# Softmax division in the layout of the values product: inverted sums spread by DMA

## The chip, the cores and the metric

The kernel runs on one core of one Trainium2 chip. The time is the device time of one execution in microseconds, the median of a few runs.

## The reference

One transformer layer on x of shape 16 x 512 x 256. Sliding-window attention with 16 heads of 16 and a window of 128: for each block of 128 queries the keys are the block itself and the one before, the scores get a bias that depends on distance, softmax is taken over the keys, and the result is projected with `w_out`. Then residual and layer norm give x1. A gated recurrence runs over the 16 sequences of x1 (`T` is the sequence number, all 512 positions at once), and its final state `c` enters every output:

```
p = softmax(scores); o = einsum(p, v)
x1 = layernorm(x + o @ w_out.T)
c = sigmoid(x1[t] @ wf.T + c @ uf.T + bf) * c + sigmoid(... wi, ui, bi) * tanh(... wc, uc, bc)   # for t in 0..15
out = layernorm(x1 + tanh(x1 @ wo.T + c @ uo.T + bo))
```

## The kernel before, in words

All is fp32; products that need full precision are made of a high part (rounded, `fp32r`) and a low part (value minus high), three matmul passes each. ScalarE makes the high parts (`x_hi`, `qk_hi`, `ot_hi`, `x1_hi`, `c_hi`), VectorE mostly the low parts by `minus_hi` (L661: `x_lo`, `qk_lo`, `ot_lo`, `x1_lo`), GpSimd the low part of the state (L364).

**Pipeline.** `iteration(t)` on each engine works on several sequences at once: q and k of t+1, scores of t, values of t-1, output projection and layer norm of t-2, gates of t-3. An iteration has 16 *slots* (`attend(0)` to `attend(15)`); slot s makes raw scores for quad s // 4 (four heads) of sequence t (TensorE, L951, into the banks `MX`), whose row maxima VectorE takes (L689, into `max_q`), and, seven slots later, the masked scores of the same piece (L972), which ScalarE exponentiates (L448) into `Pt`. GpSimd cuts the window out of `Pt` (L347, L349). Between the slots stand the other products, written out by hand in the same order on each engine; every engine waits on semaphores.

**Rows through DRAM.** q and k parts are stored to `parts_dram` by SyncE (`parts_to_dram`, four DMAs of 256 KB for each of two chunks, L239) and read back stacked (`stack`, eight DMAs for each quad, L254). Row maxima are transposed by TensorE (L959), negated into `max_rows` (L454) and put into the stack by two DMAs (`max_to_stack`, L262). SyncE works through its list in order: a wait there holds back all that stands behind it.

**The division.** The values product (L986) gives four heads at once, 32 rows a head: 16 context rows, then the row of the softmax sums (a column of ones in `Vp`), for 512 queries. `ctx_out` (L459) copies it to the single buffer `ctx_raw`. `ctx_transpose` (L994) turns it with four matmuls, so that queries lie on partitions. `normalise` on VectorE takes the reciprocal of the 16 sums a partition (L698) and multiplies (L703) into `o_tok`. With all four quads done `o_transpose` (L1027, eight matmuls) turns back, and `ot_hi` and `ot_lo` make the two parts of `oT` for the projection with `Wout`.

**Start and end.** At the start SyncE loads all weights, ScalarE and GpSimd make their parts (`weights_hi`, L416; L340), and the first exponentials wait for the fifth of them. Behind the last iteration `last_sequences()` on each engine finishes the last sequences in an order of its own; then a second phase reads x1 back from DRAM into `ring` and makes the outputs with `Wo` (L1297).

The few lines around which the change turns:

```
c4 = bank[:, :].rearrange("p (n h d) -> p n h d", n=NB, h=4)
ve.reciprocal(rden..., c4[:, :, :, D]).then_inc(rden_done, 1)
o4 = o_tok[:, :, 4 * D * g:4 * D * (g + 1)]...
ve.tensor_tensor(o4, c4[:, :, :, 0:D], r4, ALU.mult).then_inc(o_done, 1)
```

## Time and profile before

| | |
|---|---|
| time, median of 3 runs | 994.17 us (993.75 to 994.33) |
| the profiled execution, its own time | 994.83 us |
| its span, first to last instruction | 992.7 us |
| mean granted TensorE clock | 0.955 |
| TensorE busy | 911.2 us, 92% |
| VectorE busy | 714.1 us, 72% |
| ScalarE busy | 574.8 us, 58% |
| GpSimd busy | 409.0 us, 41% |
| DMA, mean over the span | 131.86 MB, 133 GB/s |

The profile is of one execution. A busy share is taken over the whole span; a stretch of the views by time shows it for one part. "Idle before" is an engine's pause in front of an instruction, with what ended it. A granted clock of 1.00 is 2.4 GHz, 0.50 is 1.2 GHz.

### The profile page before, as it was taken

The numbers are of one execution on the slowest core, as the hardware profiler recorded it, in microseconds if no ns is written. First come the engines' busy times: TensorE is split into PE (matmuls) and PEld (weight loads), VectorE is DVE, ScalarE is ACT, GpSimd is POOL, SyncE is SP. The second block draws the span as 40 slices with busy tenths as digits, with TensorE's granted clock in tenths as the row PEclk, the third lists the DMA queues.
The fourth block names the chain that finished last, engine by engine and source line by source line (L and its number), as shares of the span: only waits on it lengthen the run. The fifth ranks groups of instructions, "written<-read, shape, count | busy, mean of one in ns | idle before, by whom it ended". The sixth has DMA issues, their size and how long they took to land. (4 is left out here: it accounts for less than half of the span.)

```text
span 992.7 us, 25986 instructions
## 1 busy us (share of the span) xinstructions
PE 911.2 (92%) x9500; PEld 749.7 (76%) x9500; DVE 714.1 (72%) x2795; ACT 574.8 (58%) x1167; POOL 409.0 (41%) x687
## 2 busy tenths in 40 slices
PE   3587889999999999999999999999999999989994
PEld 2365668888888888888888888888787876668884
DVE  7666677878787868787878787878787754337875
ACT  6044556565656565656565656565656554335786
POOL 6143343444535353535353535354444443001443
PEclk8586989999999999999999999999999989899998
DMA  7644454535454545353645454645444400131764
GB/s 265 164 124 127 131 139 132 151 122 156 124 151 128 145 134 150 123 154 125 153 128 151 128 143 137 149 131 147 133 121 138 119 23 22 44 106 46 215 204 131
DMA packets 93534, 131.86 MB, mean 133 GB/s; under 512 B 12128, under 2 KB 47584, under 8 KB 93408
## 3 DMA queue, kind: packets, MB, share of 16 engines
q1 hardware_dynamic: 93136, 129.95, 45.3%
q8 instruction: 76, 1.25, 0.5%
q14 instruction: 50, 0.41, 0.1%
q10 hardware_dynamic: 272, 0.26, 0.1%
HBM read 79.31 MB, written 50.33 MB: 131 GB/s over the span
## 5 line engine op out<-in xcount | busy, mean ns | idle before, releaser
L689 DVE CUSTOM_DVE_ANT_0 bank<-bank,mask 128x256 f32<-128x256 f32 (+1 forms) x1024 | 369.4, 423 | 130.7 <-PE bank L951 128.7
L448 ACT ACTIVATE Pt<-bank 128x512 f32<-128x512 f32 (+1 forms) x512 | 248.2, 536 | 193.4 <-PE bank L972 193.3
L347 POOL TENSOR_SCALAR_AFFINE_SELECT Pt<-Pt 128x512 f32<-128x512 f32 x256 | 170.4, 666 | 403.9 <-ACT Pt L448 403.9
L951 PE MATMUL bank<-Ks,Qs 59*128 59x256 f32 (+1 forms) x1024 | 148.2, 319 | 44.9 <-DVE max_q L689 31.3
L951 PEld LDWEIGHTS bank<-Ks,Qs 59*128 59x128 f32 x1024 | 107.3, 191 | 86.6 <-DVE max_q L689 42.5
L689 DVE DVE_READ_ACCUMULATOR2_ANT max_q<- 128x1 f32 x1024 | 144.9, 142 | 0.0
L349 POOL TENSOR_SCALAR_AFFINE_SELECT Pt<-Pt 128x384 f32<-128x384 f32 x256 | 144.7, 565 | 0.0
L986 PE MATMUL bank<-Pt,Vp 128*32 128x256 f32 (+1 forms) x2048 | 130.9, 377 | 0.0
L932 PE MATMUL bank<-x1T,Wg 64*128 64x512 f32 x960 | 127.9, 398 | 1.0 <-DVE o_tok L703 1.0
L932 PE MATMUL bank<-cT,Ug 64*128 64x512 f32 x960 | 125.7, 393 | 0.0
L972 PE MATMUL bank<-Qs,Ks 60*128 60x256 f32 (+1 forms) x1024 | 111.8, 271 | 0.7 <-ACT Pt L448 0.3
L986 PEld LDWEIGHTS bank<-Pt,Vp 128*32 128x32 f32 x2048 | 81.4, 116 | 31.9 <-issue 7.9
L932 PEld LDWEIGHTS bank<-cT,Ug 64*128 64x128 f32 x960 | 89.1, 184 | 18.2
L932 PEld LDWEIGHTS bank<-x1T,Wg 64*128 64x128 f32 x960 | 87.3, 185 | 18.9 <-DVE o_tok L703 1.4
L972 PEld LDWEIGHTS bank<-Qs,Ks 60*128 60x128 f32 x1024 | 94.7, 192 | 3.0 <-issue 1.3
L459 ACT ACTIVATE ctx_raw<-bank 128x512 f32<-128x512 f32 x64 | 38.2, 597 | 53.3 <-PE bank L994 50.7
L486 ACT ACTIVATE gate<-bank,bias_half 128x512 f32<-128x512 f32 x64 | 42.4, 685 | 42.2 <-PE bank L932 23.9
L920 PE MATMUL bank<-xT,Win 128*128 128x512 f32 x204 | 55.1, 423 | 7.9 <-DVE Win L661 7.9
L932 PE MATMUL bank<-Win,xT 64*128 64x256 f32 x768 | 54.6, 284 | 0.0
L920 PEld LDWEIGHTS bank<-xT,Win 128*128 128x128 f32 x204 | 40.1, 203 | 16.6 <-DVE Win L661 7.9
L661 DVE SCALAR_TENSOR_TENSOR qk_parts<-bank,qk_parts 128x512 fp32r<-128x512 f32 x64 | 42.5, 685 | 13.9 <-ACT qk_parts L431 13.9
L431 ACT ACTIVATE qk_parts<-bank 128x512 fp32r<-128x512 f32 x64 | 38.0, 593 | 23.0 <-PE bank L920 20.2
(111 smaller groups left out, 1354.7 us busy)
## 6 DMA issues: line engine op xcount, KB each, us to landing
parts_dram<-qk_parts SPq DMA_DIRECT2D x128, 256.0 KB
Qs<-parts_dram SPq DMA_DIRECT2D x128, 128.0 KB, 2.7
Ks<-parts_dram SPq DMA_DIRECT2D x128, 128.0 KB, 2.8
xt_raw<-in_xt SPq DMA_DIRECT2D x16, 512.0 KB, 4.5
Qs<-parts_dram SPq DMA_DIRECT2D x128, 64.0 KB, 2.7
Ks<-parts_dram SPq DMA_DIRECT2D x128, 64.0 KB, 2.7
x_res<-in_x SPq DMA_DIRECT2D x16, 512.0 KB, 3.9
x_dram<-y SPq DMA_DIRECT2D x16, 512.0 KB, 4.4
```

Source lines behind the costliest of these rows:

```text
L347: gp.affine_select(out=p4[:, :, 0:128], in_=p4[:, :, 0:128], compare_op=ALU.is_ge, fill=0.0, base=0, pattern=[[0, 4], [1, 128]], channel_m ...
L349: gp.affine_select(out=p4[:, 0:3, 128:256], in_=p4[:, 0:3, 128:256], compare_op=ALU.is_ge, fill=0.0, base=0, pattern=[[0, 3], [-1, 128]], ...
L448: sc.activation(probabilities(g, 2 * pair + odd)[:, S * a:S * a + n], SC[odd][:, 0:n], ACT.Exp).then_inc(exp_done, 1)
L459: sc.activation(ctx_raw[:, :], bank[:, :], ACT.Copy).then_inc(ctx_done, 1)
L486: ins = sc.activation(gate[:, k if k == 3 else which, :], bank[:, :], ACT.Tanh, bias=bias_half[:, which, j:j + 1], scale=0.5)
L661: return ve.scalar_tensor_tensor(out_, in_, scale, hi.bitcast(F32), op0=ALU.mult, op1=ALU.subtract)
L689: ins = ve.tensor_tensor_reduce(out=raw, in0=raw, in1=mask[:, keys], scale=1.0, scalar=MASKED, op0=ALU.add, op1=ALU.max, accum_out=max_q[: ...
L920: ins = te.matmul(out_, w, m, start=(first and n == 0), stop=(last and n == len(todo) - 1))
L932: ins = te.matmul(out_, w(r), m(r), start=(turn == 0 and opens and n == 0), stop=final, skip_group_check=True)
L951: ins = te.matmul(MX[odd][:, 256 * (n % 2):256 * (n % 2) + 256][:, keys], Qs[rows, 2 * g + pair, n * WIN:(n + 1) * WIN], Ks[rows, 2 * g + ...
L972: ins = te.matmul(SC[odd][:, 256 * (j % 2):256 * (j % 2) + width], Ks[rows, 2 * g + pair, j * WIN:(j + 1) * WIN], Qs[rows, 2 * g + pair, j ...
L986: ins = te.matmul(bank[32 * hh:32 * hh + 32, j * WIN:j * WIN + width], Vp[:, j, PITCH * h:PITCH * h + 32], probabilities(g, hh)[:, 256 * j ...
```

## The change

For the first 15 sequences the context is not turned on TensorE. ScalarE copies it to `ctx_raw` as before and stores it to DRAM from its own queue (`ctx_dram`, one DMA a quad). SyncE loads the rows of the contexts into `o_un`, in the layout in which `oT` is needed, and the rows of the sums into `den_q` (four DMAs). VectorE turns 32x32 blocks of the sums, inverts them and turns back; SyncE stores the inverses and reads them back 16 times each (`inv_den`); GpSimd multiplies. `ot_hi` and `ot_lo` now read `o_un` and stand one place later, behind slots 1 and 2. The last sequence goes the old way (`last_...`).

To make room: the low parts of x move from VectorE to GpSimd, and both parts of x are made an iteration earlier, in slots 11 and 12 (x of t+2 instead of t+1 in slots 1 and 2). `Wo` and `Uo` become parts of `Win`'s memory and are loaded and split at the end, not at the start.

```
+ def load_denominators(t):
+     sp.wait_ge(den_cleared, 1)
+     for g in range(QUADS): wait(sp, ctx_stored[g], 16, t, 16)
+     wait(sp, inv_stored, 16, t - 1, 16)
+     rows = ctx_dram[t % 2].rearrange("g (h r) (q i) -> q (g h) r i", r=2 * D, i=128)[:, :, D, :]
+     for q in range(4): sp.dma_start(den_q[32 * q:32 * q + H, :], rows[q]).then_inc(den_in, 16)
+ def load_contexts(t, c):
+     for g in (2 * c, 2 * c + 1): wait(sp, ctx_stored[g], 16, t, 16)
+     wait(sp, otlo_done, 2, t - 1, c + 1)
+     rows = ctx_dram[t % 2, 2 * c:2 * c + 2].rearrange("g (h r) s -> (g h) r s", r=2 * D)[:, 0:D, :]
+     sp.dma_start(o_un[:, c, :], rows).then_inc(o_un_in[c], 16)
+ def store_inverses(t):
+     wait(sp, inv_turned, 1, t, 1)
+     sp.dma_start(inv_dram[t % 2].rearrange("r (q i) -> q r i", i=128), den_q[:, :]).then_inc(inv_stored, 16)
+ def spread_inverses(t):
+     wait(sp, inv_stored, 16, t, 16)
+     for c in range(KC):
+         wait(sp, scaled_done, 2, t - 1, c + 1)
+         rows = inv_dram[t % 2, 8 * c:8 * c + 8]
+         sp.dma_start(inv_den[:, c, :], rows.unsqueeze(1).to_broadcast([8, D, S])).then_inc(inv_in[c], 16)
  # SyncE, iteration(t)
+ if now: stack(t, 2)
+ if by_rows: load_contexts(t - 1, 0)
  if real(t + 2): load_xt(t + 2)
  if now:
-     stack(t, 2)
      max_to_stack(t, 0)
...
+ if by_rows: load_denominators(t - 1)
  if n1: stack(t + 1, 0)
+ if by_rows: load_contexts(t - 1, 1)
  if now: max_to_stack(t, 2)
+ if by_rows:
+     store_inverses(t - 1)
+     spread_inverses(t - 1)
  if n1: parts_to_dram(t + 1, 1)
+ if t == B - 1: load_last_weights()
  # GpSimd
+ def scale_contexts(t, c):        # in front of window(t + 1, 2, 0), in iteration t + 2
+     wait(pool, o_un_in[c], 16, t, 16)
+     wait(pool, inv_in[c], 16, t, 16)
+     gp.tensor_tensor(o_un[:, c, :], o_un[:, c, :], inv_den[:, c, :], ALU.mult).then_inc(scaled_done, 1)
+ x_lo(t + 2, c)                   # behind window(t, 0, 3)
  # ScalarE, ctx_out
- wait(act, ct_ready, 4, t, g)
+ wait(act, ctx_stored[pg], 16, pt, 16)
  sc.activation(ctx_raw[:, :], bank[:, :], ACT.Copy).then_inc(ctx_done, 1)
+ if t < B - 1:
+     wait(act, ctx_done, 4, t, g + 1)
+     sc.dma_start(ctx_dram[t % 2, g], ctx_raw[:, :]).then_inc(ctx_stored[g], 16)
  # ScalarE, last_sequences, in front of c_hi and layernorm of t - 1
+ last_weights_hi()                # halves Uo, rounds Wo and Uo: three operations of 128x512
  # VectorE, behind slot 13
  attend(13)
+ if p1: turn_denominators(t - 1)
  if n1: qk_lo(t + 1, 3, B1)
- if p1: normalise(t - 1, 3, A0)
+ if p1: invert_denominators(t - 1)
  if p2: x1_lo(t - 2, 0, B0)
+ if p1: turn_inverses(t - 1)
  if p2: x1_lo(t - 2, 1, B1)
```

On TensorE the four `ctx_transpose` (slots 0, 5, 8 and 13) and the two `o_transpose` (slot 0) go, and the waits on `o_done`, which freed their banks, become waits on `maxrow_done`.

SyncE, end of an iteration (iteration 3), from the row maxima of quad 2 to the next iteration's first stack; before:

```order
L262 DMA Qs<-max_rows 1x8x128 x2
L239 DMA parts_dram<-qk_parts 8x16x512 x4
L262 DMA Qs<-max_rows 1x8x128 x2
L254 DMA Qs<-parts_dram 32x2x512
L254 DMA Qs<-parts_dram 16x2x512
```

and in the change, from the load of the second contexts:

```order
L293 DMA o_un<-ctx_dram 128x1x512
L275 DMA Qs<-max_rows 1x8x128 x2
L297 DMA inv_dram<-den_q 4x32x128
L305 DMA inv_den<-inv_dram 128x1x512 x2
L252 DMA parts_dram<-qk_parts 8x16x512 x4
L275 DMA Qs<-max_rows 1x8x128 x2
L267 DMA Qs<-parts_dram 32x2x512
L267 DMA Qs<-parts_dram 16x2x512
```

The store and the two spreads of the inverses now stand between the row maxima and the parts, and the second of them waits for the first to land.

VectorE behind the maxima of slot 13, before:

```order
L661 SCALAR_TENSOR_TENSOR qk_parts<-bank,qk_parts 128x512
L698 RECIPROCAL rden<-bank 128x16
L703 TENSOR_TENSOR o_tok<-bank,rden 128x4x64
L661 SCALAR_TENSOR_TENSOR x1T<-bank,x1T 128x512 x2
L689 ISA bank,max_q<-bank,mask 128x128
```

and in the change:

```order
L799 STREAM_TRANSPOSE den_t<-den_q 128x128
L764 SCALAR_TENSOR_TENSOR qk_parts<-bank,qk_parts 128x512
L804 RECIPROCAL den_t<-den_t 128x4x16
L764 SCALAR_TENSOR_TENSOR x1T<-bank,x1T 128x512
L808 STREAM_TRANSPOSE den_q<-den_t 128x128
L764 SCALAR_TENSOR_TENSOR x1T<-bank,x1T 128x512
L792 ISA bank,max_q<-bank,mask 128x128
```

Two transposes and a reciprocal stand where one reciprocal and one product stood, the last of them between the two subtractions of x1T.

ScalarE in slots 11 to 13, before:

```order
L438 ACTIVATE Vp<-bank 128x2x16x16
L448 ACTIVATE Pt<-bank 128x384 x2
L438 ACTIVATE Vp<-bank 128x2x16x16
L431 ACTIVATE qk_parts<-bank 128x512
L454 ACTIVATE max_rows<-bank 16x128
L448 ACTIVATE Pt<-bank 128x512 x2
L431 ACTIVATE qk_parts<-bank 128x512
L459 ACTIVATE ctx_raw<-bank 128x512
L477 ACTIVATE x1T<-bank 128x512 x2
```

and in the change:

```order
L516 ACTIVATE Vp<-bank 128x2x16x16
L504 ACTIVATE xT<-xt_raw 128x512
L526 ACTIVATE Pt<-bank 128x384 x2
L516 ACTIVATE Vp<-bank 128x2x16x16
L504 ACTIVATE xT<-xt_raw 128x512
L509 ACTIVATE qk_parts<-bank 128x512
L532 ACTIVATE max_rows<-bank 16x128
L526 ACTIVATE Pt<-bank 128x512 x2
L509 ACTIVATE qk_parts<-bank 128x512
L541 ACTIVATE ctx_raw<-bank 128x512
L544 DMA ctx_dram<-ctx_raw 128x512
L577 ACTIVATE x1T<-bank 128x512 x2
```

Two conversions of x are new in front of `qk_hi`, and the store's issue in front of the copies of x1T.

## Rows read from the trace of the kernel before

**Rows 1.** The page, part 1: busy time of each engine, its share and its instructions.
```profile
PE 911.2 (92%) x9500; PEld 749.7 (76%) x9500; DVE 714.1 (72%) x2795; ACT 574.8 (58%) x1167; POOL 409.0 (41%) x687
```
**Rows 2.** Busy time by stretch; columns: stretch, its length, then each engine, clock, DMA.
```profile
110.00:160.00 50.00, 41.66 (x462) 32.51 (x457) 36.14 (x164) 27.49 (x60) 20.03 (x38) 0.90 0.48 139
...
471.00:521.00 50.00, 49.44 (x575) 41.26 (x573) 38.86 (x162) 31.09 (x66) 23.05 (x39) 1.00 0.52 139
```
**Rows 3.** TensorE in order of time, iterations 9 and 10: start, us, engine, line, what.
```profile
484.64 0.66 PE L994 MATMUL bank<-ident,ctx_raw 128*128 128x128 f32 x4
...
512.59 1.57 PE L932 MATMUL bank<-x1T,Wg 64*128 64x512 f32 x12
...
519.61 0.66 PE L994 MATMUL bank<-ident,ctx_raw 128*128 128x128 f32 x4
520.10 1.04 PE L1027 MATMUL bank<-ident,o_tok 128*128 128x128 f32 x8
521.07 0.50 PE L951 MATMUL bank<-Ks,Qs 59*128 59x256 f32 x4
...
529.80 0.72 PE L951 MATMUL bank<-Ks,Qs 59*128 59x128 f32 x4
...
534.50 0.66 PE L994 MATMUL bank<-ident,ctx_raw 128*128 128x128 f32 x4
```
**Rows 4.** VectorE in order of time, slots 12 to 14 of iteration 9.
```profile
507.20 0.69 DVE L661 SCALAR_TENSOR_TENSOR qk_parts<-bank,qk_parts 128x512 fp32r<-128x512 f32 x1 [0.94 <-ACT qk_parts L431]
...
510.70 1.35 DVE L661 SCALAR_TENSOR_TENSOR x1T<-bank,x1T 128x512 fp32r<-128x512 f32 x2
```
**Rows 5.** ScalarE in order of time, slot 13 of iteration 9, slot 1 of 10.
```profile
509.58 0.60 ACT L459 ACTIVATE ctx_raw<-bank 128x512 f32<-128x512 f32 x1 [0.40 <-PE bank L994]
510.07 1.26 ACT L477 ACTIVATE x1T<-bank 128x512 fp32r<-128x512 f32 x2
...
521.84 1.08 ACT L448 ACTIVATE Pt<-bank 128x512 f32<-128x512 f32 x2
```
**Rows 6.** SyncE's DMA issues in order of time, end of iteration 9, start of 10.
```profile
496.44 2.81 SPq L262 DMA_DIRECT2D Qs<-max_rows  x2
...
509.51 3.29 SPq L239 DMA_DIRECT2D parts_dram<-qk_parts  x4
518.95 1.36 SPq L262 DMA_DIRECT2D Qs<-max_rows  x2
520.42 1.79 SPq L254 DMA_DIRECT2D Qs<-parts_dram  x4
```
**Rows 7.** The tile Qs: from issue to landing of its DMAs.
```profile
DMA to landing us min/median/max: 2.2/2.7/4.9
```
**Rows 8.** The last sequences in order of time, ScalarE, then TensorE.
```profile
843.87 2.07 ACT L470 ACTIVATE y<-y,shift,rstd 128x256 f32<-128x256 f32 x4
...
846.08 1.94 PE L1040 MATMUL bank<-ident,y 128*128 128x128 f32 x8 [3.99 <-ACT y L470]
```
**Rows 9.** ScalarE's queue at the start: what issuing one DMA takes.
```profile
0.78 0.48 ACTq L600 DMA_DIRECT2D Pt<-in_w_in  x1
```
**Rows 10.** Groups by line and shape: count, busy us, mean ns, idle before, releaser.
```profile
L364 POOL TENSOR_TENSOR cT<-c,cT 128x512 fp32r<-128x512 f32 x26 | 32.8, 1280 | 0.0
...
L703 DVE TENSOR_TENSOR o_tok<-bank,rden 128x256 f32<-128x256 f32 x64 | 27.2, 425 | 12.3 <-PE bank L1027 10.6
...
L661 DVE SCALAR_TENSOR_TENSOR xT<-xt_raw,xT 128x512 fp32r<-128x512 f32 x32 | 22.8, 716 | 4.7 <-ACT xT L426 4.7
...
L698 DVE RECIPROCAL rden<-bank 128x16 f32<-128x16 f32 x64 | 15.9, 249 | 41.9 <-PE bank L994 41.9
...
L661 DVE SCALAR_TENSOR_TENSOR cT<-c,cT 128x512 fp32r<-128x512 f32 x8 | 10.1, 1288 | 2.1 <-ACT cT L613 1.2 <-ACT cT L494 0.9
```
**Rows 11.** Busy time by stretch in iteration 15; columns as in rows 2.
```profile
800.00:805.00 5.00, 3.06 (x27) 2.29 (x23) 3.37 (x19) 2.94 (x6) 3.58 (x8) 0.86 0.00 0
805.00:810.00 5.00, 5.00 (x43) 3.23 (x41) 1.44 (x9) 1.31 (x4) 0.45 (x1) 0.50 0.01 2
```

More of the change, by code:

```diff
@@ L263, in max_to_stack, with load_last_weights @@
                                  max_rows[8 * odd:8 * odd + 8, :].bitcast(F32)).then_inc(maxrow[g], 16)
+            def load_denominators(t):
+                sp.wait_ge(den_cleared, 1)
+                for g in range(QUADS):
+                    wait(sp, ctx_stored[g], 16, t, 16)
+                wait(sp, inv_stored, 16, t - 1, 16)
+                rows = ctx_dram[t % 2].rearrange("g (h r) (q i) -> q (g h) r i", r=2 * D, i=128)[:, :, D, :]
+                for q in range(4):
+                    sp.dma_start(den_q[32 * q:32 * q + H, :], rows[q]).then_inc(den_in, 16)
+            def load_contexts(t, c):
+                for g in (2 * c, 2 * c + 1):
+                    wait(sp, ctx_stored[g], 16, t, 16)
+                wait(sp, otlo_done, 2, t - 1, c + 1)
[10 more added lines that the diff above has]
+                    sp.dma_start(inv_den[:, c, :], rows.unsqueeze(1).to_broadcast([8, D, S])).then_inc(inv_in[c], 16)
+            def load_last_weights():
+                sp.wait_ge(xlo_done, 2 * B)
+                for n, w in enumerate((w_o, u_o)):
+                    sp.dma_start(out_stage[:, n, :].rearrange("p (c n) -> p c n", c=KC), w.rearrange(v, p=128)).then_inc(last_weights_in, 16)
             def load_xt(t):
@@ L270, in iteration @@
                 p1, p2, n1, now = real(t - 1), real(t - 2), real(t + 1), real(t)
+                by_rows = p1 and t - 1 < B - 1
                 if p1: max_to_stack(t - 1, 3)
@@ L299, in _ @@
             sp.wait_ge(xt_ready, 2 * B)
+            sp.wait_ge(last_lo, 2)
             def load(t, i):
@@ L364, in c_lo, with x_lo @@
                 gp.tensor_tensor(cT[:, 1, j, :], c2[:, j, :], cT[:, 0, j, :].bitcast(F32), ALU.subtract).then_inc(clo_done, 1)
+            def x_lo(t, c):
+                wait(pool, xhi_done, 2, t, c + 1)
+                gp.tensor_tensor(xT[:, t % 2, 1, c, :], xt_raw[:, c, :], xT[:, t % 2, 0, c, :].bitcast(F32), ALU.subtract).then_inc(xlo_done, 1)
+            def scale_contexts(t, c):
+                wait(pool, o_un_in[c], 16, t, 16)
+                wait(pool, inv_in[c], 16, t, 16)
+                gp.tensor_tensor(o_un[:, c, :], o_un[:, c, :], inv_den[:, c, :], ALU.mult).then_inc(scaled_done, 1)
             def iteration(t):
                 p1, p2, now = real(t - 1), real(t - 2), real(t)
+                if p2 and t - 2 < B - 1:
+                    for c in range(KC):
+                        scale_contexts(t - 2, c)
                 if p1:
@@ L384, in iteration @@
                         window(t, 0, hh)
+                    if real(t + 2):
+                        for c in range(KC):
+                            x_lo(t + 2, c)
                     for hh in range(4):
@@ L389, in _ @@
                 iteration(t)
+                if t == B:
+                    for n, w in enumerate((Wo, Uo)):
+                        pool.wait_ge(last_hi, n + 1)
+                        gp.tensor_tensor(w[:, 1, :, :], out_stage[:, n, :].rearrange("p (c n) -> p c n", c=KC),
+                                         w[:, 0, :, :].bitcast(F32), ALU.subtract).then_inc(last_lo, 1)
             def second(t, rnd, i):
@@ L606, in _ @@
                 qk_hi(0, k, banks[4 + (k + 2) % 4])
-            act.wait_ge(weights_in, 80)
-            for n in range(5):
+            act.wait_ge(weights_in, 48)
+            for n in range(3):
                 weights_hi(n)
@@ L1022, in project_qk, with last_o_transpose @@
                                      for c in range(KC)], qk_ready)
-            def o_transpose(t, c, bank):
-                wait(pe, o_done, 4, t, 4)
+            def last_o_transpose(c, bank):
+                pe.wait_ge(o_done, 4)
                 for n in range(NB):
-                    ins = te.transpose(bank[:, WIN * n:WIN * (n + 1)], o_tok[:, n, 128 * c:128 * c + 128], ident[:, :])
+                    ins = te.transpose(bank[:, WIN * n:WIN * (n + 1)], last_o_tok[:, n, 128 * c:128 * c + 128], ident[:, :])
                 ins.then_inc(ot_ready, 1)
@@ L1212, in last_sequences @@
                 scores(t, 2, 3)
+                wait(pe, gate_done, 6, t - 2, 1)
                 project_out(t - 1, 0, B0)
+                wait(pe, gate_done, 6, t - 2, 2)
                 project_out(t - 1, 1, B1)
@@ L1224, in last_sequences @@
                 scores(t, 3, 2)
-                wait(pe, o_done, 4, t, 2)
-                ctx_transpose(t, 2, MX[0])
+                pe.wait_ge(o_done, 2)
+                last_ctx_transpose(2, MX[0])
                 scores(t, 3, 3)
@@ L1236, in last_sequences @@
                 gate_of_input(t - 1, 1, A1)
-                wait(pe, o_done, 4, t, 3)
-                ctx_transpose(t, 3, MX[0])
+                pe.wait_ge(o_done, 3)
+                last_ctx_transpose(3, MX[0])
                 gate_of_state(t - 1, 0, A0)
```

192 lines of the change are left out of this document (107 added, 85 removed).

## The prediction

> **What bounds the kernel now.** I read five views, in this order. The page's busy shares first: TensorE is busy for 911.2 us of 992.7, 92%, and VectorE for 72% [rows 1]. Busy shares are averages, so next the same sums by stretch. From 471 to 521 us TensorE is busy for 49.44 of 50 us at a granted clock of 1.00; from 110 to 160 us only for 41.66, at 0.90, with VectorE a little less busy too, 36.14 against 38.86 [rows 2]. So from iteration 3 on what TensorE has to do is the time, and in iterations 1 and 2 the exchange between raw scores and their maxima is. Third, TensorE in order of time: the transpose of a context at 484.64 comes again at 534.50, so one iteration is 49.86 us [rows 3]. Fourth, VectorE, ScalarE and SyncE in the same iteration, for what each does behind slot 13, where the change puts its new work [rows 4 to 6]. Last, the time from a DMA's issue to its landing [rows 7], the last sequences [rows 8], the start [rows 9] and what one instruction of a kind takes [rows 10].
>
> **The change part by part.**
>
> *Transposes leave TensorE.* A context transpose of four matmuls delays the next group by 0.49 us (519.61 to 520.10) [rows 3]; four of them are 2.0 us. The two output transposes take 0.97 us (520.10 to 521.07) [rows 3]. Together 2.97 us per sequence, for 15 of 16 sequences. At 49.44 of 50 us busy TensorE waits for nothing else in these places, so in iterations 3 to 14, twelve of them, I count all of it.
>
> *VectorE sheds* four reciprocals of 0.249, four products of 0.425 and two subtractions of 0.716 (xT) per iteration [rows 10], 4.1 us, and gets two transposes of 128x128 and a reciprocal of 128x64. No row shows a VectorE transpose; between the reciprocal of 128x16 (0.249) and the subtraction of 128x512 (0.716 [rows 10]) I take 0.3, near the smaller one, since 128 columns are nearer to 16 than to 512. Net minus 3.2 us. In the saturated iterations that is worth nothing by itself: TensorE hides it.
>
> *Behind slot 13 a new stall.* TensorE opens the input half of the next gates at 512.59; VectorE's two x1T subtractions, which it needs, start at 510.70 and take 1.35, so they end 0.6 us before [rows 3, 4]. Now ScalarE converts x of sequence t+2 in slots 11 and 12 (two of about 0.6); one is hidden in front of an exponential, the other makes `qk_hi`, for which VectorE already waits 0.94 us [rows 4], some 0.25 later. VectorE's three small operations instead of reciprocal and product add 0.9 - 0.67 = 0.2, and the turn between the two subtractions and its waits another 0.2. ScalarE's store of the context (0.48 us to issue one [rows 9]) stands in front of the x1T copies, but the wait of 0.40 for the context's transpose goes [rows 5], so plus 0.1. And TensorE arrives 0.5 earlier, having no transpose in slot 13. 0.6 - 0.25 - 0.2 - 0.2 - 0.1 - 0.5 is about -0.7: a stall of 0.7 us an iteration, from 0 (every addition covered) to 1.5 (transposes at 0.716).
>
> *SyncE's queue.* On the clock of the rows the inverses are turned at about 512.1. The store lands 2.7 us after its issue [rows 7], 514.9; two spreads take 0.5 each to issue (one ordinary DMA is 0.45: four are 1.79 [rows 6]), 516; the parts, which left at 509.51, take their 3.29, until 519.3; the row maxima behind them 1.36, or 2.81 as at 496.44, where they also stood right behind parts; then eight DMAs of the stack of quad 1, 3.6 us, until 524.3 to 525.7, the last landing 2.3 later, 526.6 to 528.0 [rows 6, 7]. Slot 4 needs them at 529.80 [rows 3], and comes 1.46 (slot 0) + 0.5 - 0.7 = 1.3 earlier, at 528.5. So 0.5 to 1.9 us of room is left of over 3; with landings that reach 4.9 [rows 7] the stall is between 0 and 2 us, and I take 0.3, near the lower end, because the median landing leaves room. The row maxima among these, of the last quad, are needed one slot earlier, in slot 3, and leave by 522.
>
> *GpSimd* gets four products or subtractions of 128x512, 1.28 each [rows 10], 5.1 us in 50, where it is busy for 23.05 [rows 2]. The product with the inverses must be done before ScalarE's conversion in slot 1. Store 2.7, spread 0.5 + 0.5 + 2.7, two products 2.6: 9 us from 512.1, so 521.1. ScalarE wants it when its exponentials of slot 1 are done, 521.84 + 1.08 [rows 5] less 1.3 for the shorter slots, 521.6. It is covered, by 0.5 us, and behind it VectorE's own subtraction waits until slot 2's maxima are done, a slot later. I cost it at nothing; without the cover the oT parts, and with them TensorE's projection in slot 3, would be late by what the DMAs take over 2.7.
>
> *The other DMAs* (four loads of denominators, two of contexts, each about 0.45) fill SyncE's pauses between the stacks. Nothing; without that cover 2.7 us on SyncE, and the stack of the next sequence late.
>
> *Outside iterations 3 to 14.* Iterations 1 and 2 have both cuts on the path: 2.0 and 2.97 of TensorE and up to 3.2 of VectorE; I take 3.5 each, 7 in all (4 to 10). Iteration 15: 2.5. The output transposes of sequence 14, behind the loop: 1. Start: three ScalarE operations on 128x512 of about 0.6 (the context's copy takes 0.60 [rows 5]) and two loads fewer; the first raw scores wait for DMA anyway, so 1 (0 to 1.5). End: ScalarE converts the last weights, three of about 0.57 (0.60 less their overlap), in front of the layer norm at 843.87, for which TensorE sat idle for 3.99 us [rows 8]: plus 1.7, all on the path.
>
> *Sum.* 12 x (2.97 - 0.7 - 0.3) = 24, plus 2.5 + 7 + 1 + 1 - 1.7 = 9.8: 33.8 us. The profiled execution took 994.83 us (span 992.7, 2.1 around it), so 961.0; the runs' median, 994.17, is 0.7 lower: **960.4 us**.
>
> **The rivals.**
>
> *A. The stack comes late.* One more DMA latency on SyncE (landings of 4 to 4.9 instead of 2.7, parts issued slower behind a full queue) turns the room of slot 4 into a stall of 1 to 2 us an iteration: 969 to 981 us. For it: issues right behind parts took twice as long [rows 6]. Against: around 512 the queue is otherwise empty. The Trainium skill speaks for it: "DMA: Bandwidth & Descriptors", § Rules, says that an outermost dimension below 16 confines a DMA to that many engines, and the store's is 4, the spread's 8; with the page's 27 GiB/s an engine, an estimate of 0.6 us for the store and 1.1 for each spread on top of the latency would make the queue's 0.3 about 0.7 and the sum 965. No row here shows it.
>
> *B. Slower: the clock follows the stall.* If the chain from the turned inverses to slot 4 is over 2 us longer than I count, TensorE idles long enough for the clock to fall. From 800 to 805 it was busy for 3.06 of 5 us, and in the next 5 us the clock was 0.50, the 1.2 GHz level [rows 11]; what takes 3 us at full clock then takes 6. A stall of 2.5 and 3 of slow clock, 5.5 + 0.7, against 2.97, is 3.2 lost an iteration: 12 x 3.2 - 9.8 = 29 lost, 1023 us. Against: the 0.4 us stalls within 471 to 521 leave the clock at 1.00 [rows 2].
>
> *C. No stall.* Both new chains fit: 12 x 2.97 = 35.6 and 9.8, with up to 4 more at the ends: 945 to 949 us.
>
> *D. VectorE blocked by GpSimd.* VectorE's cT subtractions at the start, with two SBUF operands, took 1.288 on average, against 0.716 for xT's of the same shape; at the start GpSimd subtracts weights beside them [rows 10]. The oT subtraction now reads two SBUF operands too, and GpSimd has 5.1 us more. Two operations an iteration at plus 0.6, half of it on the path: 968 us. By the Trainium skill, "SBUF — State Buffer", that is an exclusive lock between a VectorE instruction with two SBUF inputs and a GpSimd one that reads SBUF; the row agrees.
>
> *E. It moves nothing* (transposes were hidden): the row at 1.00 clock and 49.44 of 50 busy excludes it all but wholly.
>
> **How the numbers follow.** Forecast (952 to 968) 0.50, A 0.20, B 0.12, C 0.10, D 0.06, E 0.02. Within 0.2% (2 us) a measurement of this kernel can't tell a change. The range runs from the upper part of C to A's upper end, 948 to 980; it leaves out B, E and most of C, in all some 2 in 10. Faster 0.86, same 0.02, slower 0.12.
>
> **What would show it.** Period of an iteration 47.9 us; no matmul on ctx_raw or the output before the last sequence; TensorE idle about 0.7 in slot 14, released by VectorE's x1T, and up to 0.3 in slot 4, released by DMA to Ks or Qs; clock 1.00 in the middle; the wait for the layer norm at the end 5.7 instead of 3.99. A stall over 1 us in slot 4 would be A; clock below 0.97 in the middle, B.

## The result, and the profile after

The changed kernel takes **1025.55 us** (median of 4 runs, 1021.04 to 1028.11), the kernel before beside it 994.25 (993.75 to 996.83). The ratio is 1.0305, 95% interval 1.0263 to 1.0346: 3% slower, where 960.4 was forecast. The profiled execution took 1028.11 us. One execution of one kernel below, turned_early_SyncE_as_is, was disturbed and took 3334.88 us; its time is that of its three others, and it has no trace to read.

The page of the changed kernel, parts 1, 3 and 4:
```profile
span 1026.4 us, 25344 instructions
...
PE 885.1 (86%) x9140; PEld 727.2 (71%) x9140; DVE 685.8 (67%) x2693; ACT 574.5 (56%) x1167; POOL 485.0 (47%) x745
...
q1 hardware_dynamic: 105196, 147.16, 52.0%
...
PE 17%; SPq 6%; DMA 6%; ACT 6%; DVE 5%; issue 2%; POOL 2%; ACTq 0%; DVEq 0%; POOLq 0%
```
Against [rows 1] TensorE is 26.1 us less busy, with 360 matmuls fewer, and VectorE 28.3. The span grew by 33.7 all the same, so TensorE now stands still for 59.8 us more. SyncE's queue and the DMAs, hardly on the chain of waits before, hold 12% of it. What TensorE waited for from 175 to 805 us (us in total, times, longest):
```profile
PE bank L1091 <- DMA Qs<-max_rows: 21.6, 18, 4.3
PE bank L1070 <- DMA Ks<-parts_dram: 13.9, 11, 2.0
PE bank L1159 <- DVE qk_parts L764: 13.1, 12, 1.2
PE bank L1070 <- DVE max_q L792: 5.3, 12, 0.4
```
In the kernel before the first of these groups was 0.3 us, the second and third were absent, and the last was 7.7. The busy time by stretch (columns as in [rows 2]), after:
```profile
75.00:125.00 50.00, 40.35 (x373) 28.88 (x365) 27.60 (x138) 22.93 (x49) 21.21 (x36) 0.76 0.51 152
125.00:175.00 50.00, 40.57 (x414) 32.62 (x415) 30.90 (x140) 25.14 (x53) 23.06 (x40) 0.83 0.67 174
175.00:805.00 630.00, 571.98 (x6622) 473.24 (x6622) 443.99 (x1872) 372.79 (x772) 335.90 (x504) 0.99 0.63 174
```
and of the kernel before, in the same stretches:
```profile
75.00:125.00 50.00, 40.03 (x372) 29.56 (x372) 31.69 (x149) 25.06 (x53) 17.79 (x32) 0.80 0.47 129
125.00:175.00 50.00, 45.79 (x504) 37.17 (x504) 36.14 (x163) 27.84 (x58) 19.41 (x36) 0.93 0.47 136
175.00:805.00 630.00, 619.36 (x7206) 513.45 (x7202) 490.15 (x2055) 388.94 (x805) 291.49 (x486) 1.00 0.48 136
```
As the mark of an iteration I take the end of VectorE's x1T subtractions (512.05 in [rows 4]). Between the 2nd and the 14th mark an iteration takes 50.03 us before and 52.16 after: 12 x 2.13 = 25.6 of the 33.7 us. The first mark came at 162.33 and comes at 169.25, 6.9 more, and the period behind it adds 0.8. All that follows adds 0.4 together.

In these twelve periods as a whole (the stretch between the marks; before, then after):
```profile
212.25:812.62 600.37, 590.33 (x6833) 488.47 (x6832) 462.60 (x1939) 368.02 (x763) 273.72 (x457) 0.99 0.47 134
...
219.95:845.92 625.97, 567.54 (x6548) 470.18 (x6544) 439.29 (x1858) 367.57 (x761) 332.41 (x501) 0.98 0.62 170
```
TensorE is busy for 22.8 us less and idle for 48.4 us more (10.0 before, 58.4 after): together the 25.6.

SyncE at the end of iteration 9, beside [rows 6]:
```profile
529.63 1.30 SPq L275 DMA_DIRECT2D Qs<-max_rows  x2
532.68 0.56 SPq L297 DMA_DIRECT2D inv_dram<-den_q  x1
535.24 1.27 SPq L305 DMA_DIRECT2D inv_den<-inv_dram  x2
536.63 3.87 SPq L252 DMA_DIRECT2D parts_dram<-qk_parts  x4
540.55 3.67 SPq L275 DMA_DIRECT2D Qs<-max_rows  x2
544.32 2.52 SPq L267 DMA_DIRECT2D Qs<-parts_dram  x4
546.88 1.83 SPq L267 DMA_DIRECT2D Ks<-parts_dram  x4
```
Before, the parts left 1.7 us behind the start of the third quad's row maxima; now it is 7.0. The row maxima of the fourth quad, which come right behind the parts, take 3.67 us to issue for 1.36. TensorE, in slot 4 of two iterations and in slot 13:
```profile
500.83 0.50 PE L1070 MATMUL bank<-Ks,Qs 59*128 59x128 f32 x4 [1.21 <-DMA Ks<-parts_dram]
...
531.49 0.66 PE L1159 MATMUL bank<-ident,y 128*128 128x128 f32 x4 [1.17 <-DVE qk_parts L764]
...
551.60 0.50 PE L1070 MATMUL bank<-Ks,Qs 59*128 59x128 f32 x4 [1.08 <-DMA Ks<-parts_dram]
```
The 21.6 us for row maxima are not all of one place. By their distance from the mark, 10.0 (7 times) fell in slot 3, for the fourth quad's, 6.8 (8 times) in slot 11, for the second quad's, 4.3 (once) in slot 7, for the first quad's, and 0.5 in slot 15. The first of these, and the 13.9 for the parts in slot 4, wait for what follows the second chunk's parts on SyncE; the other 11.6 have other places in its list.

The groups by line and shape for what is new on GpSimd and VectorE (busy us, mean ns, idle before, releaser), and the wait at the end that answers to [rows 8]:
```profile
L431 POOL TENSOR_TENSOR o_un<-o_un,inv_den 128x512 f32<-128x512 f32 x30 | 39.5, 1316 | 70.8 <-DMA inv_den<-inv_dram 70.8
...
L764 DVE SCALAR_TENSOR_TENSOR oT<-o_un,oT 128x512 fp32r<-128x512 f32 x30 | 25.0, 871 | 0.6 <-ACT oT L550 0.6
...
L804 DVE RECIPROCAL den_t<-den_t 128x64 f32<-128x64 f32 x15 | 8.0, 534 | 0.0
L799 DVE STREAM_TRANSPOSE den_t<-den_q 128x128 f32<-128x128 f32 x15 | 4.6, 307 | 0.0
...
880.38 1.94 PE L1159 MATMUL bank<-ident,y 128*128 128x128 f32 x8 [5.55 <-ACT y L570]
```

### The profile page after: what moved, and what is told of

It reads as the page before. It is cut to its first block and busy times, and to the rows that moved or that the text cites. A ratio compares the mean times of both kernels' runs of the same rounds, so it can differ in the third digit from the quotient of the medians.

```text
span 1026.4 us, 25344 instructions
## 1 busy us (share of the span) xinstructions
PE 885.1 (86%) x9140; PEld 727.2 (71%) x9140; DVE 685.8 (67%) x2693; ACT 574.5 (56%) x1167; POOL 485.0 (47%) x745
## 2 busy tenths in 40 slices
DMA packets 114232, 164.77 MB, mean 161 GB/s; under 512 B 14588, under 2 KB 52924, under 8 KB 114108
## 5 line engine op out<-in xcount | busy, mean ns | idle before, releaser
L1070 PE MATMUL bank<-Ks,Qs 59*128 59x256 f32 (+1 forms) x1024 | 144.6, 322 | 58.9 <-DMA Ks<-parts_dram 31.1
L1051 PEld LDWEIGHTS bank<-x1T,Wg 64*128 64x128 f32 x960 | 91.7, 186 | 18.2 <-issue 4.7
L1051 PEld LDWEIGHTS bank<-cT,Ug 64*128 64x128 f32 x960 | 94.2, 185 | 13.8
L431 POOL TENSOR_TENSOR o_un<-o_un,inv_den 128x512 f32<-128x512 f32 x30 | 39.5, 1316 | 70.8 <-DMA inv_den<-inv_dram 70.8
L1039 PE MATMUL bank<-xT,Win 128*128 128x512 f32 x204 | 56.0, 428 | 10.2 <-DVE Win L764 8.6
```

Of the source, the lines that this page charges most:

```text
L431: gp.tensor_tensor(o_un[:, c, :], o_un[:, c, :], inv_den[:, c, :], ALU.mult).then_inc(scaled_done, 1)
L1039: ins = te.matmul(out_, w, m, start=(first and n == 0), stop=(last and n == len(todo) - 1))
L1051: ins = te.matmul(out_, w(r), m(r), start=(turn == 0 and opens and n == 0), stop=final, skip_group_check=True)
L1070: ins = te.matmul(MX[odd][:, 256 * (n % 2):256 * (n % 2) + 256][:, keys], Qs[rows, 2 * g + pair, n * WIN:(n + 1) * WIN], Ks[rows, 2 * g + ...
```

## The experiments

Three theories. **Queue:** what SyncE waits for and issues in front of the second chunk's parts (the turned inverses, their store's round trip, the spread) makes parts, row maxima and stack late. **Traffic:** the 33 MB more (164.8 for 131.9) slow every transfer. **Chain:** the new work in slots 11 to 13 makes the queries' low part late. Where only a median is given, the ratio's interval is in the table at the end of this section. The edits are shortened.

### The inverses' chain left out; then the contexts' DMAs too

```diff
-  if by_rows: load_denominators(t - 1)
-  if by_rows: store_inverses(t - 1); spread_inverses(t - 1)
-  wait(pool, inv_in[c], 16, t, 16)
-  turn_denominators / invert_denominators / turn_inverses
```


> Left out of the changed kernel: the loads of the sums, VectorE's two turns and the inversion, the store and the spread; GpSimd multiplies the contexts by ones (so the output is not divided). The stores and loads of the contexts stay. Changed kernel: 1025.6 us, of which TensorE waits 21.6 for row maxima, 13.9 for the parts in slot 4 and 13.1 for the second x1 transpose from 175 to 805 us. Queue theory (what SyncE waits for and issues in front of the second chunk's parts makes them, the row maxima and the stack late): both DMA waits all but vanish, and with them the turn's share of the third: 1025.6 - 35 - 5 to 10, about 980 to 985. Traffic theory (the 33 MB more, three quarters of them contexts, make every transfer late): a quarter of the 35.5 us of DMA waits goes, 1010 to 1015. Chain theory (the loss is in slot 13 on VectorE and ScalarE): 10 us, 1015, with the DMA waits as they are.

Second kernel: also no `sc.dma_start(ctx_dram...)` and no `load_contexts`.

> As the run without the inverses, and the stores and loads of the contexts left out too: GpSimd multiplies a constant, so the output is not the attention's. All transposes of contexts and outputs are gone from TensorE and nothing is added to any DMA queue. All theories that put the loss on DMAs: the whole saving shows, 994.2 - 26 (TensorE's busy time less) - what the x1 transposes still wait, 960 to 968. If ScalarE's x conversions in slots 11 and 12 alone hold up the chain of slot 13, the wait for the second x1 transpose stays near 1 us an iteration and the time is at the upper end, 972 or above. Against the run without the inverses: queue theory 10 to 20 us less, traffic theory 45 to 50 less.

Measured: 977.5 and 974.4 us. The chain of the inverses costs 48 us, and the contexts, some 24 of the 33 MB (155.4 MB are left without the inverses), cost 3, no more than these runs scatter. Traffic as the theory had it falls. TensorE's waits without the inverses:
```profile
PE bank L1152 <- DVE qk_parts L760: 10.3, 12, 1.0
...
PE bank L1084 <- DMA Qs<-max_rows: 5.5, 6, 1.8
```
The waits for the parts are gone and 16 of the 21.6 us for row maxima too; the wait in slot 13 has lost only 2.8.

### Which part of the chain: bytes or waits

```diff
-  sp.dma_start(inv_den[:, c, :], rows.unsqueeze(1).to_broadcast([8, D, S]))
+  sp.dma_start(inv_den[:, c, 0:64], rows.unsqueeze(1).to_broadcast([8, D, 64]))
```


> The changed kernel with every wait and every DMA in its place, but the spread brings 64 of the 512 columns (64 KB instead of 512 KB a sequence; the other columns of the multiplier are ones, so the output is not divided there). The run without the whole chain of the inverses took 977.5 us and the changed kernel 1025.6: 48 us between them. If the time of the chain is in what SyncE waits for and in the order (VectorE's turn back, then the store's round trip, then the parts), nothing changes: 1015 to 1026. If it is in the spread's bytes, whose 8 MB stand in the same queue ahead of the parts, the row maxima and the stack, most of the 48 go: 980 to 992.

The other half: the spread alone, its source `x[0, 16*c:16*c+16, :]`, with no wait for `inv_stored`.

> The opposite part: no loads of the sums, no turns, no inversion, no store and no wait for its landing, but the whole spread, 2 DMAs of 256 KB in front of the parts, from rows of the input (the output is not the attention's). If the time is in the waits and the order: near the run without the chain, 977 to 985 (two issues, 1.3 us, are left in front of the parts). If it is in the bytes: 1005 to 1025. What this one and the thin spread leave of the 48 us together shows whether the two causes add.

Measured: 1000.2 and 979.3 us. The bytes alone cost 2 us, the waits, turns and small DMAs alone 23, both together 48. They don't add: each makes the other dear. The thin spread takes off bytes but not packets (114232, as in the changed kernel); the spread alone has 4081 packets more than the run without the chain (110331 for 106250), and costs its 2 us with them. In the thin spread TensorE still waited:
```profile
PE bank L1161 <- DVE qk_parts L765: 12.3, 12, 1.2
PE bank L1072 <- DMA Ks<-parts_dram: 9.4, 12, 1.6
PE bank L1093 <- DMA Qs<-max_rows: 8.0, 6, 3.2
```
All six waits for row maxima are in slot 11 here, none in slot 3. Waits in slot 11 are in every run without the transposes: 3.0 us with none of the change's DMAs, 5.0 without the inverses, 6.8 in the changed kernel.

### SyncE's order: parts first

```diff
+  if n1: parts_to_dram(t + 1, 1)
   if by_rows:
       store_inverses(t - 1)
       spread_inverses(t - 1)
-  if n1: parts_to_dram(t + 1, 1)
```


> Only SyncE's order is changed: the second chunk's parts are stored ahead of the wait for the inverted sums, their store and the spread. Queue theory: the parts leave 4 us earlier, TensorE's 13.9 us in slot 4 go, and some of the 21.6 us for row maxima, which now stand behind the store's round trip as before: 1003 to 1012. Traffic theory: nothing, 1020 to 1028. The product on GpSimd starts 4 us later; if that is what the kernel cannot bear, slot 3's output projection waits and the time is above 1028.

1061.3 us: the queue theory's number was wrong, since what it took to be free had a deadline of its own. The waits for the parts all but go (1.2 us are left), but the product is 4 us later, and now ScalarE stands still for it, and TensorE for ScalarE's exponentials:
```profile
ACT oT L550 <- POOL o_un L431: 76.4, 24, 5.5
...
PE bank L1091 <- ACT Pt L526: 35.1, 12, 5.7
```
In the changed kernel ScalarE waited for no product. With the parts first the granted clock was 0.95 from 175 to 805 us, so the stalls cost more than their own length. So the store and the spread could not simply go behind the parts: both orders miss one of two deadlines.

### The row maxima on ScalarE's queue

```diff
   sc.activation(max_rows[:, :], bank[0:16, 0:128], ...)
+  wait(act, maxrow_done, 4, t, g + 1)
+  for odd in range(2): sc.dma_start(Qs[r:r + 1, ...], max_rows[8 * odd:8 * odd + 8, :])
```
(and `max_to_stack` taken from SyncE)

> The two DMAs that bring a quad's row maxima into the stack are issued by ScalarE right behind the copy that makes them, on its own queue, and by SyncE no longer. Queue theory: TensorE's 21.6 us for row maxima go all but a few, and SyncE is 2 to 3 us an iteration earlier for the parts; ScalarE pays 8 issues of 0.4 an iteration, most of it beside TensorE: 995 to 1005. Traffic theory, if the transfers share 16 engines whatever the queue: the maxima still land late behind bulk, over half of the 21.6 us stay, 1012 to 1025.

1090.7 us, outside what either theory gave. ScalarE in order of time:
```profile
524.38 0.25 ACT L520 ACTIVATE max_rows<-bank 16x128 fp32r<-16x128 f32 x1
524.67 2.08 ACTq L524 DMA_DIRECT2D Qs<-max_rows  x2
526.80 0.87 ACT L514 ACTIVATE Pt<-bank 128x384 f32<-128x384 f32 x2 [2.16 <-issue]
```
TensorE waits for no row maxima any more, but from 175 to 805 us ScalarE stands for 81.9 us behind its own issues (113.7 over the whole span), and TensorE 39.4 us for exponentials (23 times), at a granted clock of 0.93. I had counted 0.4 an issue from a queue that was free; two small ones took 1.31 and 2.08 us in this trace. The Trainium skill, "DMA: Bandwidth & Descriptors", § Issuing engines are not separate DMA queues, says that starting DMAs on several engines at once only saves the time of the sequencer that starts them, which it calls usually small relative to the DMA itself. In this trace that time is 0.9 us a row maxima DMA on average, and it decides; whether nothing else is saved no run here isolates.

### The sums turned earlier

```diff
   attend(12)
+  if p1: turn_denominators(t - 1); invert_denominators(t - 1); turn_inverses(t - 1)
   if n1: qk_lo(t + 1, 2, B0)
```
(the same three calls behind slot 13 are gone)
```diff
   if n1: stack(t + 1, 0)
+  if by_rows: store_inverses(t - 1)
   if by_rows: load_contexts(t - 1, 1)
   if now: max_to_stack(t, 2)
-  if by_rows: store_inverses(t - 1)
   if by_rows: spread_inverses(t - 1)
```


> The whole change, but VectorE turns, inverts and turns back behind slot 12, in front of the low part of the queries, where it waits 1.35 us for ScalarE anyway; SyncE issues the store right behind the next sequence's first stack, in front of the contexts' second load and the third row maxima, and the spread stays in front of the parts. The parts then leave some 4 us earlier than in the changed kernel (532.5 for 536.6 in the iteration that was read) and the product on GpSimd starts 2.5 us earlier too. Theory of the waits and the order: most of the 48 us come back, 980 to 992, which would be the first whole version under the kernel before. Theory of the bytes: 1010 to 1026, as the same 33 MB move. If the sums land after slot 12, VectorE stands still there and the maxima behind it are late: above 1000 by another wait, TensorE's for max_q.

**985.7 us, ratio 0.9904 (0.9871 to 0.9937)**: it computes everything, moves the same bytes, and is faster than the kernel before. SyncE, at the end of iteration 9:
```profile
511.05 0.56 SPq L297 DMA_DIRECT2D inv_dram<-den_q  x1
...
512.39 1.33 SPq L275 DMA_DIRECT2D Qs<-max_rows  x2
514.15 1.26 SPq L305 DMA_DIRECT2D inv_den<-inv_dram  x2
515.53 4.75 SPq L252 DMA_DIRECT2D parts_dram<-qk_parts  x4
522.76 1.39 SPq L275 DMA_DIRECT2D Qs<-max_rows  x2
```
The store's round trip now lies under the contexts' load and the row maxima, and behind the parts there are 2.5 us of pause before the fourth quad's row maxima, which again take 1.39 us.

> Half of the run with the sums turned early (985.7 us): VectorE turns behind slot 12, but SyncE's order is that of the changed kernel (first stack, contexts' second load, third row maxima, store, spread, parts). The store then leaves when the row maxima are issued, about 531 instead of 532.7 in the iteration read, and its landing is still waited for with nothing in between. Theory of the waits in front of the parts: of the 4 us that the parts were early there, about 2 are left, so a time between 986 and 1025, 1000 to 1010. If only VectorE's chain of slot 13 counted, 986; if only SyncE's order did, 1020.

1012.3 us with VectorE's half of the move alone (1008.9 to 1017.6), a little above the 1000 to 1010 expected. 13 of the 40 us come from turning earlier, 27 only when SyncE has other issues under the round trip.

> The run with the sums turned early (985.7 us), with the spread behind the parts instead of in front of them. The parts leave 1.3 us earlier still, and the product on GpSimd starts some 4 us later, about where the changed kernel has it (539 in the iteration read). If the product has that slack, nothing waits for it on ScalarE, the row maxima of the fourth quad are behind the same issues, and the time is 980 to 987. If the product then comes too late for ScalarE (as in the run with the parts in front of both the store and the spread, 1061 us), TensorE waits for the exponentials in slot 4 and the time is 1000 to 1030.

1000.0 us (989.6 to 1006.6). From 175 to 805 us ScalarE waited 36.1 us for the product, 26 times. The product has no slack, even from its earlier start.

### The conversions of x

```diff
   v_out(t, 0, A0)
-  if real(t + 2): x_hi(t + 2, 0)
   attend(12)
   v_out(t, 1, A1)
-  if real(t + 2): x_hi(t + 2, 1)
   ...
   attend(14)
+  if real(t + 2): x_hi(t + 2, 0); x_hi(t + 2, 1)
```
(and GpSimd's `x_lo` behind the last `window(t, 1, hh)`)

> The run with the sums turned early (985.7 us), and the inputs of the sequence after next converted later: ScalarE's two copies behind slot 14 (where it waits 2.5 us for scores) instead of behind slots 11 and 12, GpSimd's low parts behind the last window. In every run with the change's order TensorE waits 0.7 to 1.1 us an iteration for the second x1 transpose (13.8 us there), in the kernel before never. If ScalarE's two copies of 0.64 us in front of the copy of the queries are the cause, this wait goes: 985.7 - 8 to 13, 973 to 978. If it is the shorter stretch on TensorE (the o transposes no longer stand ahead), it stays, 984 to 988. GpSimd reaches the product about 1.5 us later; if that has no slack, ScalarE waits for the product and the time is above 990.

988.6 us, no different from 985.7: the intervals overlap. The wait in slot 13 fell from 13.8 to 8.3 us, not to nothing, and the row maxima took some of it back (7.5 to 9.6).

> The kernel before with this part of the change alone: inputs are converted for the sequence after next, ScalarE's copies behind slots 11 and 12, the low parts on GpSimd. Nothing else is moved, and the transposes of contexts and outputs stay on TensorE. If the two copies make the queries' low part late, the second x1 transpose waits 0.5 to 1 us an iteration: 994.3 + 6 to 12, 1000 to 1006. If the copies only show because TensorE is faster in the changed order, it is hidden here: 992 to 996.

997.9 us, ratio 1.0027 (1.0005 to 1.0050). On the kernel before the move makes a wait of 4.2 us, 11 times. So the copies account for about 0.4 us an iteration of the wait in slot 13. The run without context DMAs, which has the copies, no turns and a TensorE without transposes, has 0.8; the changed kernel, with the turns, 1.1. The chain theory is right that this wait exists, and it is 13 us of it, not the loss.

### What the lateness of the parts costs by itself

```diff
+  wait(sp, x1lo_done, 2, t - 2, 1)
+  sp.dma_start(scratch, ident[0:32, :]).then_inc(came_back, 16)
+  sp.wait_ge(came_back, 16 * (t - 1))
   parts_to_dram(t + 1, 1)
```
(three such round trips in the runs "later")

> The kernel before, with nothing of the change but one wait on SyncE: in front of the second chunk's parts it waits for VectorE's first x1 low part (about when the change's turn back ends), stores 16 KB of a constant to DRAM and waits until they have landed, as the changed kernel waits for its inverses. No bulk is added, TensorE keeps its transposes. The theory of the wait in front of the parts: the stack is late in slot 4 and row maxima are late in slots 3 and 11, TensorE waits 1 to 2 us an iteration there and the kernel takes 1006 to 1020. If the kernel before has slack there, because its TensorE reaches slot 4 about 3 us later behind the transposes: 994 to 998. If only wait and bytes together hurt (the thin spread alone cost 23 of 48): also near 996 to 1000.

> The kernel before with three such round trips one after another in front of the parts, some 7 us later than without, and TensorE's transposes in place. SyncE stood idle 6.1 us behind these parts in the kernel before, until the fourth quad's row maxima. Theory of the slack: with 7 us the parts' issues reach into the row maxima's place, 1 to 3 us a stack and row maxima late, 1000 to 1030. If the parts' lateness alone does nothing at all in this kernel: 995 to 998.

> The run without any of the change's DMAs (974.4 us; TensorE without the transposes of contexts and outputs), and in front of the second chunk's parts the same one wait as in the run on the kernel before that cost it nothing (995.8 for 995.0): VectorE's first x1 low part, then a store of 16 KB and its landing. There it made the parts 3.4 us later. Theory that the slack in front of the parts is set by when TensorE reaches slots 3 and 4, which is 3 us earlier without the transposes: TensorE waits 0.5 to 1.5 us an iteration for the parts or the row maxima, 980 to 992. Theory that the wait is harmless until the queue carries the contexts, sums and inverses as well: 974 to 977.

> The run without any of the change's DMAs (974.4 us) with three round trips in front of the second chunk's parts, as in the run on the kernel before that took them without loss (996.4 for 994.5). The parts' issue then starts some 5 us behind VectorE's second x1 low part (changed kernel 4.2, kernel before -1.5, the run with one round trip 1.0), so this run has the changed kernel's lateness, and none of its bulk. Theory that the transposes on TensorE were the slack: TensorE waits for row maxima in slot 3 or the parts in slot 4, 1 to 2 us an iteration, 985 to 1000. Theory that lateness only hurts beside the bulk of contexts and inverses: 971 to 977.

Measured: 995.8 and 996.4 on the kernel before (ratios 1.0009 and 1.0009), 971.6 and 981.1 without the transposes and the bulk. Read from SyncE in order of time, means over 12 iterations, us behind the mark:

| run | parts start | 4th maxima start, end | last stack issue of quad 1 | us |
|---|---|---|---|---|
| kernel before | -2.8 | 6.9, 8.3 | 12.5 | 994 |
| before_parts_late | 1.0 | 6.9, 8.3 | 12.4 | 995.8 |
| before_parts_later | 4.0 | 7.4, 10.2 | 14.4 | 996.4 |
| no_dmas_parts_late | 0.4 | 6.9, 8.3 | 12.4 | 971.6 |
| no_dmas_parts_later | 3.4 | 7.3, 9.8 | 14.0 | 981.1 |
| sums_turned_early | 0.0 | 7.1, 8.5 | 12.6 | 985.7 |
| thin_spread | 3.3 | 6.9, 10.2 | 14.6 | 1000.2 |
| changed kernel | 3.5 | 7.7, 10.8 | 15.7 | 1025.6 |

Up to a start of about 1.0 the lateness costs nothing, in either order: the fourth row maxima are not ready before 6.9. From 3.3 on they stand right behind the parts and take 2.6 to 3.2 us to issue for 1.4, and the stack leaves 2 us late. The kernel before takes even that: its slot 4 comes at 17.75 (529.80 - 512.05 of [rows 3, 4]), of which 1.46 us are the transposes of slot 0. Without the transposes the kernel is at the limit: 981.1 for 974.4, and a wait for parts in 4 of the iterations:
```profile
PE bank L1067 <- DMA Ks<-parts_dram: 5.2, 4, 1.7
```
With the contexts and the small DMAs beside it (thin spread) every iteration is over it, and with the whole spread in front of the parts, 1.1 us further. How the last 25 us divide between that, transfers in a full queue and a lower clock stays open. One case of the latter is the longest wait, in slot 7: SyncE issued the first quad's row maxima at 448.86, right behind the loads of contexts and of x, and TensorE had them only at 461.01:
```profile
461.01 0.57 PE L1091 MATMUL bank<-Qs,Ks 60*128 60x256 f32 x4 [4.30 <-DMA Qs<-max_rows]
```
with the DMA engines full (share 1.07, 1.06 and 0.97 in the three 5 us behind 445). Behind this stall the granted clock was 0.66 for 5 us:
```profile
455.00:460.00 5.00, 1.71 (x18) 1.23 (x14) 4.72 (x13) 0.02 (x1) 1.40 (x3) 1.00 0.97 181
460.00:465.00 5.00, 3.99 (x23) 3.26 (x24) 0.00 (x0) 3.04 (x6) 0.00 (x0) 0.66 0.53 145
```
The mean of 0.99 from 175 to 805 us hides what this costs. The next longest waits of that stretch are these:
```profile
602.06 0.79 PE L1091 MATMUL bank<-Qs,Ks 60*128 60x256 f32 x4 [3.21 <-DMA Qs<-max_rows]
...
785.35 0.63 PE L1091 MATMUL bank<-Qs,Ks 60*128 60x256 f32 x4 [2.86 <-DMA Qs<-max_rows]
```
Behind them the clock was 0.62 and 0.69 in the 5 us from 600 and from 605, and 0.66 in those from 785. The periods with the three waits, and a quiet one between:
```profile
427.67:482.93 55.26, 48.41 (x550) 40.41 (x550) 36.65 (x157) 31.18 (x65) 28.49 (x43) 0.97 0.64 165
...
583.24:637.97 54.73, 49.32 (x550) 41.62 (x550) 37.10 (x157) 30.95 (x65) 28.01 (x43) 0.94 0.59 166
637.97:688.80 50.83, 47.23 (x552) 38.73 (x550) 36.78 (x157) 30.86 (x65) 27.98 (x43) 1.00 0.66 185
...
740.58:796.44 55.86, 48.70 (x551) 39.87 (x550) 36.88 (x157) 30.18 (x63) 25.47 (x41) 0.97 0.58 159
```
In the eight periods at 1.00 TensorE is busy for 46.8 to 47.2 us, 47.0 on average, so these three have 5.5 us of busy time more for the same matmuls. The run without any of the change's DMAs, between the same marks:
```profile
212.24:790.12 577.88, 554.93 (x6544) 464.15 (x6544) 427.81 (x1822) 365.79 (x761) 334.70 (x501) 1.00 0.50 140
```
The changed kernel is busy for 12.6 us more than that (567.5): these 5.5, 3.5 in the last period, where the clock was 0.93 (as in the kernel before) and there 1.00, and 3.6 in small pieces that no row explains.

| run | median us | ratio to before, 95% |
|---|---|---|
| no_dmas_parts_late | 971.6 | 0.9762 (0.9728 to 0.9796) |
| no_context_dmas | 974.4 | 0.9785 (0.9746 to 0.9825) |
| no_inverses | 977.5 | 0.9813 (0.9787 to 0.9839) |
| spread_only | 979.3 | 0.9832 (0.9798 to 0.9866) |
| no_dmas_parts_later | 981.1 | 0.9849 (0.9818 to 0.9879) |
| **sums_turned_early** | 985.7 | 0.9904 (0.9871 to 0.9937) |
| x_converted_late | 988.6 | 0.9932 (0.9896 to 0.9968) |
| before_parts_late, _later | 995.8, 996.4 | 1.0009 (0.9993 to 1.0026), 1.0009 (0.9991 to 1.0028) |
| before_x_moved | 997.9 | 1.0027 (1.0005 to 1.0050) |
| early_spread_last | 1000.0 | 1.0033 (1.0002 to 1.0064) |
| thin_spread | 1000.2 | 1.0044 (1.0015 to 1.0074) |
| turned_early_SyncE_as_is | 1012.3 | 1.0169 (1.0113 to 1.0226) |
| the change | 1025.6 | 1.0305 (1.0263 to 1.0346) |
| parts_first | 1061.3 | 1.0638 (1.0575 to 1.0701) |
| maxima_by_ScalarE | 1090.7 | 1.0936 (1.0895 to 1.0976) |

## Why the prediction was wrong

**Transposes leave TensorE: right.** 2.97 us an iteration forecast. Without any of the new DMAs an iteration takes 48.16 us (50.03 before), with 1.1 us of waits that the kernel before had not: 1.87 + 1.1 = 3.0. The busy time says nearly the same: at a clock of 1.00 a period has 49.2 to 49.5 us of it before and 46.4 to 46.7 in that run, some 2.8 less.

**The stall behind slot 13: the size nearly, the place wrong.** 0.7 forecast, released by the x1T subtraction; 13.1 / 12 = 1.1 measured, one step earlier: the second x1 transpose waits for the bank that the queries' low part frees. The reciprocal took 534 ns for my 0.3 us; the two turns 0.3 each, as taken.

**SyncE's queue: the step that failed.** I forecast 0.3 us an iteration; TensorE waits (21.6 - 0.3 + 13.9) / 12 = 2.9, of which 2.0 are in slots 3 and 4, where I looked, and 0.9 in slots 7, 11 and 15, which the forecast had at nothing. The start of the parts was forecast well: 516 on the clock of the rows, 3.95 behind the mark of 512.05, and 3.5 was measured. What failed is what stood behind it, each issue at its price in a queue that is free: parts 3.29 (3.8 measured), row maxima 1.36 with 2.81 only as the upper end (3.1), the stack 3.6 (4.9 with its gaps). The landing was nearly as taken, 2.8 to 3.0 us from the issue at the median for 2.7. Together the last stack issue was forecast at 12.3 to 13.7 and came at 15.7, where at most 1.9 us of room was counted. [Rows 6] showed it: row maxima behind parts had taken 2.81 at 496.44, and with the parts moved against the fourth row maxima that was no longer an upper end but the case. The same queue also waited 39.3 us for contexts to be stored, which the step on the other DMAs put at nothing. With the inverses' chain left out, the two groups cost 5.5 us, 0.5 an iteration.

**The clock behind the stalls: left out of the sum.** I counted a stall at its own length. Of the 35.4 us of busy time that left with the transposes (590.3 to 554.9), 12.6 came back, 1.05 an iteration. With it the account closes: 1.97 us an iteration were to be gained and 2.13 were lost, 4.1 apart, of which the queue is 2.6, slot 13 0.4 and this 1.05.

**GpSimd covered: right, by luck.** ScalarE waited for no product. I gave the cover 0.5 us; the run with the parts first made the product 4 us later and lost 36 us more. This margin and the one of the parts share one queue, and I had weighed them one by one.

**Outside iterations 3 to 14: wrong by some 15 us at the start.** I forecast 8 us less up to the first mark; it was 6.9 more. Even without any DMA the first mark came at 164.30, for 162.33, with TensorE idle for about as long (46 us up to 170, before 45) and busy for 129.0 of 175 us (130.1) with fewer matmuls: what was taken away came back as a lower granted clock, 0.74 from 75 to 125 us for 0.80, and 0.84 for 0.93 in the 50 behind. The marks of four kernels in the order of before lie between 162.3 and 167.0, so of the 6.9 only a part is the change's. The end, 1.7 us more forecast, had the wait of 5.55 for 3.99 as foreseen, and its period, the 14th to the 15th mark, took 37.8 us for 36.8; all behind the 14th mark took 180.5 for 180.1.

**The rivals.** A was the mechanism: stalls in slots 4 and 3 of 2.0 us an iteration, its upper end. Its time, 981 at most, left out the other slots and the clock. The rule of the Trainium skill on the outermost dimension, "DMA: Bandwidth & Descriptors", § Rules for kernel authors, which spoke for it, is not what decided: the store went out at 532.68 and the next issue followed 2.6 us later, no slower than the 2.7 I had taken from [rows 7], and the spread's bytes alone cost 2 us. B had the sign and nearly the number, 1023, the number by luck: it had a slow clock in every iteration, 3.2 us lost in each, and the clock fell behind the three longest stalls, 0.97, 0.94 and 0.97 in their periods. D shows in the row of the oT subtraction, 871 ns for 682 from a bank, and TensorE waited for none of it. The lock that the Trainium skill gives for it, "SBUF — State Buffer", § SBUF: two separate sides, would make such a row longer, as it is; nothing more here bears on it.

The gain thus went in four ways: of some 36 us that the transposes were worth, 13 went to the wait in slot 13, 35 to row maxima and parts, 13 to busy time that came back, most of it at a lower clock, and the start gave back what it should have gained and more.

## What to carry to other kernels

On a queue that issues in order, two transfers with deadlines of their own are one budget: put a wait on one and compute when the last issue behind it leaves, with the issue times of a full queue, not the median ones. Before inserting a store and a load that depends on it, look for the issues that can lie between the two; here that choice, with VectorE's work one slot earlier, turned 3% slower into 1% faster. A shorter path on the bounding engine also brings its deadlines forward, so slack is to be read against the new schedule. And a long stall can cost more than its length, by the clock behind it.
